# Softmax probabilities scaled on GpSimd before the transposes, instead of scaling the attention output

## The reference

```python
q = (query @ wq); k = (key @ wk); v = (value @ wv)     # heads of 128, rope on q and k
scores = jnp.einsum('bhqd,bhkd->bhqk', q, k) / scale
attn = jax.nn.softmax(scores + m[:, None, :, :], axis=-1)
out = jnp.einsum('bhqk,bhkd->bhqd', attn, v)
return out.reshape(bs, sq, HQ * DV) @ wo
```

## Time and profile before

| | us |
|---|---|
| three runs | 713.92, 716.35, 716.79 |
| median | 716.35 |
| the profiled execution | 712.92 |
| its span, first to last instruction | 711.2 |
| busy PE, PEld, DVE | 697.0, 592.6, 549.5 |
| busy ACT, POOL | 395.2, 300.5 |

### The profile page before, as it was taken

How to read it: one execution, slowest core, us unless ns; L and a number is a source line. 1 busy time by engine, 2 the same in 40 slices (tenths; PEclk the granted TensorE clock), 3 DMA queues, 4 the chain that set the end, 5 groups by cost and what they waited for, 6 DMA issues and landing times.

```text
span 711.2 us, 12231 instructions
## 1 busy us (share of the span) xinstructions
PE 697.0 (98%) x4085; PEld 592.6 (83%) x4085; DVE 549.5 (77%) x1175; ACT 395.2 (56%) x603; POOL 300.5 (42%) x151
## 2 busy tenths in 40 slices
PE   8999999999999999999999999999999999999986
PEld 7888888888888888888888888879989999999975
DVE  5988578658748857866865874767999999999994
ACT  4563454535546446345553654654867667676752
POOL 2353223404504503331340440200388887888780
DMA  8702022021001102202102100832887878788600
GB/s 310 271 30 75 1 74 74 0 74 59 15 22 59 66 0 74 74 0 74 64 9 74 59 0 0 348 157 79 338 292 285 339 301 340 298 336 301 282 7 16
DMA packets 20293, 93.77 MB, mean 132 GB/s; under 512 B 2608, under 2 KB 3760, under 8 KB 11440
## 3 DMA queue, kind: packets, MB, share of 16 engines
q1 hardware_dynamic: 20272, 93.50, 35.5%
HBM read 93.17 MB, written 0.33 MB: 131 GB/s over the span
## 4 chain that ended last, share of the span: by engine, by line
PE 91%; DVE 4%; DMA 3%; issue 1%; ACT 1%; SPq 0%; POOLq 0%; POOL 0%; DVEq 0%
PE bank L389 24%; PE bank L391 22%; PE bank L390 22%; PE bank L608 10%; PE bank L516 5%; PE bank L687 3%; DMA w_hs_sb<-in_w_hs 1%; DMA wqo_raw<-in_wq 1%; PE bank L487 1%; PE bank L396 1%; DVE decay L1291 1%; PE bank L443 1%; PE bank L696 1%; PE bank L659 1%; PE bank L736 1%
## 5 line engine op out<-in xcount | busy, mean ns | idle before, releaser
L1448 POOL TENSOR_TENSOR wqo_lo<-wqo_raw,wqo_hi 128x2048 fp32r<-128x2048 f32 x15 | 69.6, 4640 | 192.3 <-ACT wqo_hi L744 163.6
L1121 DVE TENSOR_TENSOR pt_lo<-bank,pt_hi 128x512 fp32r<-128x512 f32 x128 | 87.6, 689 | 51.6 <-ACT pt_hi L818 50.8
L818 ACT ACTIVATE pt_hi<-bank 128x512 fp32r<-128x512 f32 x128 | 75.6, 597 | 57.0 <-PE bank L516 57.0
L1435 POOL TENSOR_TENSOR k_lo<-rope_a,k_hi 128x512 fp32r<-128x512 f32 x32 | 42.8, 1338 | 104.2 <-ACT k_hi L762 104.2
L1082 DVE CUSTOM_DVE_ANT_0 probs<-bank,mask_sb 128x512 f32<-128x512 f32 x128 | 82.0, 686 | 0.1
L1481 POOL TENSOR_TENSOR w_out_lo<-w_out_sb,w_out_hi 128x2048 fp32r<-128x2048 f32 x16 | 73.5, 4591 | 16.2 <-ACT w_out_hi L931 16.2
L1486 POOL TENSOR_TENSOR w_gate_lo<-w_gate_sb,w_gate_hi 128x2048 fp32r<-128x2048 f32 x15 | 69.3, 4618 | 18.0 <-ACT w_gate_hi L923 18.0
L516 PEld LDWEIGHTS bank<-ident_r,probs_r 128*128 128x128 f32 x512 | 55.8, 140 | 19.2 <-DVE pt_lo L1121 5.1
L808 ACT ACTIVATE probs<-probs,neg_max 128x2048 f32<-128x2048 f32 x31 | 61.9, 2001 | 0.9 <-DVE neg_max L1072 0.8
L608 PE MATMUL bank<-xnT,w_hs_sb 128*128 128x128 f32 x512 | 60.6, 277 | 1.0 <-DMA w_hs_sb<-in_w_hs 1.0
L516 PE MATMUL bank<-ident_r,probs_r 128*128 128x128 f32 x512 | 57.8, 238 | 1.5 <-DVE pt_lo L1121 1.5
(11 more groups left out here) (193 smaller groups left out, 1728.2 us busy)
## 6 DMA issues: line engine op xcount, KB each, us to landing
w_hs_sb<-in_w_hs SPq DMA_DIRECT2D x16, 1024.0 KB, 4.8
w_gate_sb<-in_w_gate SPq DMA_DIRECT2D x16, 1024.0 KB, 4.8
w_out_sb<-in_w_out SPq DMA_DIRECT2D x16, 1024.0 KB, 6.3
wqo_raw<-in_wq SPq DMA_DIRECT2D x8, 1024.0 KB, 4.7
wqo_raw<-in_wo SPq DMA_DIRECT2D x8, 1024.0 KB, 4.8
decay<-decay_rows SPq DMA_DIRECT2D x16, 512.0 KB, 6.8
ctx_raw<-in_ctx_t SPq DMA_DIRECT2D x3, 1024.0 KB, 11.2
wk_raw<-in_wk SPq DMA_DIRECT2D x8, 256.0 KB, 2.7
```

Source lines behind the costliest of these rows:

```text
L818: act.activation(pt_hi[t % 3], ring_b[(t + 1) % 2][:, :], ACT.Copy).then_inc(s["pt_hi_ready"], 1)
L1121: dve.tensor_tensor(pt_lo[t % 3], ring_b[(t + 1) % 2][:, :], pt_hi[t % 3].bitcast(F32), ALU.subtract)\
L1448: pool.tensor_tensor(wqo_lo[:, :, :], wqo_raw[:, :, :], wqo_hi[:, :, :].bitcast(F32), ALU.subtract)\
```

## The change

In the first seven head groups VectorE inverts each head's row sum by itself (`inverse_row`, a 128 x 1 reciprocal), GpSimd multiplies that head's 128 x 2048 probabilities by it in place (`normalise`), and TensorE's transposes wait for this (`probs_normed`) where they waited for the exponentials. The two diagonals, the two broadcast matmuls, ScalarE's copy and `scale_out` are left out in these groups. `attn_high` and `attn_low` read `pv_bank`. The last group keeps the old way.

```diff
 def transpose_probs(g, t, last_head):
     if t == 0:
-        pe.wait_ge(s["probs_ready"], HG * (g + 1) - last_head)
+        if last_head:
+            pe.wait_ge(s["probs_ready"], HG * G - 1)
+        else:
+            pe.wait_ge(s["probs_normed"], HG * (g + 1))
...
-        if t == sum_steps(last_head)[2]:
-            if first_head(g) or not isinstance(g, int):
-                pe.wait_ge(s["ones_r_ready"], 1)
-            pe.wait_ge(s["diag_ready"], g + 1)
+        if last_head and t == SUM_STEPS[2]:
+            pe.wait_ge(s["ones_r_ready"], 1)
+            pe.wait_ge(s["diag_ready"], 1)
             pe.matmul(oq_bank..., ones_r, diag_hi...)
             pe.matmul(oq_bank..., ones_r, diag_lo...)
...
 def attn_high(g):
-    act.wait_ge(s["attn_out_ready"], g + 1)
-    act.activation(attn_hi[...], probs[:, 1, 0:512], ACT.Copy)
+    act.wait_ge(s["pv_ready"], g + 1)
+    act.activation(attn_hi[...], pv_bank[:, :], ACT.Copy)
...
 def q_and_k(g):
+    inverse_row(g - 1, 0)
+    inverse_row(g - 1, 1)
     k_rotate(g, 0)
+    inverse_row(g - 1, 2)
+    inverse_row(g - 1, 3)
     q_rotate(g)
     k_rotate(g, 1)
...
+def inverse_row(g, h):
+    dve.wait_ge(s["probs_ready"], HG * g + h + 1)
+    dve.reciprocal(inv_row[:, h:h + 1], row_sum[:, h:h + 1]).then_inc(s["inv_row_ready"], 1)
...
 pt_low(g, False)
-scale_out(g)
 v_low(g + 1, 0)
 attn_low(g)            # now reads pv_bank
...
+def normalise(g, h):
+    pool.wait_ge(s["inv_row_ready"], HG * g + h + 1)
+    keep_wait_apart(pool)
+    pool.tensor_scalar(probs[:, h, :], probs[:, h, :], inv_row[:, h:h + 1], None, ALU.mult)\
+        .then_inc(s["probs_normed"], 1)
...
 with pool.Fori(1, G) as g:
     split_wk(g)
     wqo_low(s["wq_hi_ready"], s["wq_lo_ready"], g)
     split_wv(g)
-    k_low(g)
+    normalise(g - 1, 0)
+    normalise(g - 1, 1)
+    k_low(g, 0)
+    normalise(g - 1, 2)
+    k_low(g, 1)
+    normalise(g - 1, 3)
+    k_low(g, 2)
+    k_low(g, 3)
     wqo_low(s["wo_hi_ready"], s["wo_lo_ready"], g - 1)
```

More of the change, by code:

```diff
@@ L53 @@
 LOWEST = -3.4028234663852886e38
-def sum_steps(last_head):
-    return (11, 12, 14, 15) if last_head else (1, 4, 7, 8)
+SUM_STEPS = (11, 12, 14, 15)
 def at_least(eng, sem, count):
@@ L150, in build @@
         row_sum = sb("row_sum", [P, HG], F32, attn)
+        inv_row = sb("inv_row", [P, HG], F32, attn)
         inv_hi = sb("inv_hi", [P, HG], F32R, attn)
@@ L256, in build @@
             qT_lo_ready vproj_ready v_copied vT_mm v_hi_ready v_lo_ready scores_ready scores_masked neg_max_ready
-            probs_ready pT_mm pt_hi_ready pt_lo_ready pv_ready inv_sum_ready inv_hi_ready inv_lo_ready diag_ready
+            probs_ready inv_row_ready probs_normed pT_mm pt_hi_ready pt_lo_ready pv_ready inv_sum_ready inv_hi_ready inv_lo_ready diag_ready
             bcast_mm bcast_ready attn_out_ready oproj_ready res_added small_in dequant_in dt_in gate_in0 gate_in1
@@ L750, in attn_high @@
             def attn_high(g):
-                act.wait_ge(s["attn_out_ready"], g + 1)
-                act.activation(attn_hi[:, :, :].rearrange("p h t -> p (h t)"), probs[:, 1, 0:512], ACT.Copy)\
+                act.wait_ge(s["pv_ready"], g + 1)
+                act.activation(attn_hi[:, :, :].rearrange("p h t -> p (h t)"), pv_bank[:, :], ACT.Copy)\
                     .then_inc(s["attn_hi_ready"], 1)
@@ L818, in pt_high @@
                     act.activation(pt_hi[t % 3], ring_b[(t + 1) % 2][:, :], ACT.Copy).then_inc(s["pt_hi_ready"], 1)
-                    if t == sum_steps(last_head)[3]:
-                        act.wait_ge(s["bcast_mm"], g + 1)
+                    if last_head and t == SUM_STEPS[3]:
+                        act.wait_ge(s["bcast_mm"], 1)
                         act.activation(probs[:, 2, 0:512], oq_bank[:, :], ACT.Copy).then_inc(s["bcast_ready"], 1)
@@ L880, in _ @@
             for i in range(2):
-                act.wait_ge(s["attn_out_ready"], G + i)
+                act.wait_ge(s["attn_out_ready"], i + 1)
                 act.activation(attn_hi[:, 2 * i:2 * i + 2, :].rearrange("p h t -> p (h t)"),
@@ L1090, in mask_scores, with last_inverse_sums, last_inverse_sums_low @@
                 row_max(g, HG - 1)
[L1092 to L1100, removed]
+            def inverse_row(g, h):
+                dve.wait_ge(s["probs_ready"], HG * g + h + 1)
+                dve.reciprocal(inv_row[:, h:h + 1], row_sum[:, h:h + 1]).then_inc(s["inv_row_ready"], 1)
+            def last_inverse_sums():
+                dve.wait_ge(s["probs_ready"], HG * G - 1)
+                dve.wait_ge(s["last_exp"], KB)
+                dve.tensor_reduce(row_sum[:, HG - 1:HG], block_max[:, HG - 1, :], X_AXIS, ALU.add)\
+                    .then_inc(s["last_sum_ready"], 1)
+                dve.wait_ge(s["last_sum_ready"], 1)
                 dve.reciprocal(inv_sum, row_sum[:, :]).then_inc(s["inv_sum_ready"], 1)
-                dve.wait_ge(s["inv_sum_ready"], g + 1)
+                dve.wait_ge(s["inv_sum_ready"], 1)
                 dve.tensor_scalar(inv_hi[:, :], inv_sum, 1.0, None, ALU.mult).then_inc(s["inv_hi_ready"], 1)
-                dve.wait_ge(s["inv_hi_ready"], g + 1)
+                dve.wait_ge(s["inv_hi_ready"], 1)
                 dve.tensor_tensor(inv_lo, inv_sum, inv_hi[:, :].bitcast(F32), ALU.subtract)\
                     .then_inc(s["inv_lo_ready"], 1)
-                dve.wait_ge(s["k_lo_ready"], KB * (g + (1 if last_head else 2)))
+                dve.wait_ge(s["k_lo_ready"], KB * G)
                 dve.tensor_tensor(diag_hi[:, :, :], ident[:, :].unsqueeze(1).broadcast_to([P, HG, P]),
                                   inv_sum.unsqueeze(2).broadcast_to([P, HG, P]), ALU.mult)
-            def inverse_sums_low(g):
-                dve.wait_ge(s["inv_lo_ready"], g + 1)
-                dve.wait_ge(s["pT_mm"], KT * g + 1)
+            def last_inverse_sums_low():
+                dve.wait_ge(s["inv_lo_ready"], 1)
+                dve.wait_ge(s["pT_mm"], KT * (G - 1) + 1)
                 dve.tensor_tensor(diag_lo, ident[:, :].unsqueeze(1).broadcast_to([P, HG, P]),
@@ L1122, in pt_low @@
                         .then_inc(s["pt_lo_ready"], 1)
[L1123 to L1132, removed]
+                    if last_head and t == SUM_STEPS[0]:
+                        last_inverse_sums()
+                    if last_head and t == SUM_STEPS[1]:
+                        last_inverse_sums_low()
             def add_out(g):
@@ L1140, in attn_low @@
                 dve.wait_ge(s["attn_hi_ready"], g + 1)
-                dve.tensor_tensor(attn_lo[:, :, :].rearrange("p h t -> p (h t)"), probs[:, 1, 0:512],
+                dve.tensor_tensor(attn_lo[:, :, :].rearrange("p h t -> p (h t)"), pv_bank[:, :],
                                   attn_hi[:, :, :].rearrange("p h t -> p (h t)").bitcast(F32), ALU.subtract)\
@@ L1197, in _ @@
             pt_low(G - 1, True)
-            dve.wait_ge(s["bcast_ready"], G)
+            dve.wait_ge(s["bcast_ready"], 1)
             dve.wait_ge(s["pv_ready"], G)
@@ L1429, in split_weight, with k_low @@
                     .then_inc(lo_done, 1)
[L1431 to L1437, removed]
+            def k_low(g, b):
+                blk = slice(b * 512, (b + 1) * 512)
+                pool.wait_ge(s["k_hi_ready"], KB * g + b + 1)
+                pool.tensor_tensor(k_lo[:, blk], rope_a[:, (b + 1) % 2, :], k_hi[:, blk].bitcast(F32), ALU.subtract)\
+                    .then_inc(s["k_lo_ready"], 1)
+            def normalise(g, h):
[3 more added lines that the diff above has]
+                    .then_inc(s["probs_normed"], 1)
             def split_wk(g):
@@ L1467, in _ @@
             split_wv(0)
-            k_low(0)
+            for b in range(KB):
+                k_low(0, b)
             with pool.Fori(1, G) as g:
```

## The result

The changed kernel takes 787.41 us (median of four runs, 786.08 to 788.38) against 715.41 for the kernel before in the runs measured with it: ratio 1.1017, interval 1.0984 to 1.105. The forecast was 723.5 and slower, the range 712 to 738. The sign was right, the size was wrong by a factor of ten (72 us against 7).

What follows compares the result with a forecast made beforehand. TensorE's matmuls were taken as the bound. Stalls of 0.52 and 1.03 less 0.53 saved gave +1.0 us an iteration, +7.1 for seven: 723.5 against the median 716.35, range 712 to 738.

Steps and rivals of the forecast that it cites:

- The bound, the saving: TensorE's matmuls bound the loop; leaving out the broadcast matmuls saves 0.53 us an iteration, 3.7 for seven.
- The lock: A VectorE addition of two SBUF tiles meeting a running GpSimd instruction waits for its end, then needs 0.55 us more.
- steps 2 to 4: Held VectorE rotation additions cost TensorE 0.52 us before turning q and 1.03 at the third turned block, each iteration.
- step 3: At q's rotation, its addition waits for GpSimd's K low part, hiding the reciprocals; q ends at 232.15 against 231.63.
- D: Time of one GpSimd normalise of 2048 columns, taken as 1.9 us from the cast, bounds 1.89 and 4.58.
- Step 5: TensorE's new wait for probs_normed: head 3 done at 239.65, TensorE there at 240.42 + 0.52, so no cost.
- rival D: A slower GpSimd normalise: at 3 us each, +23, 746; at 4.58 TensorE waits for head 3, over 770; chance 0.12.
- The sum's formula: Cost of the held additions per iteration, 3D - 4.15 us, with D the time of one GpSimd normalise.
- A: VectorE's additions get past a running normalise, both stalls vanish and 3.7 us stay as gain: 712.6; chance 0.21.
- B: Near cancellation: normalise takes 0.9 to 1.7 us, or a margin behind k_rotate(3) was counted too low: 716; chance 0.14.
- C: GpSimd keeps the lock, so q's addition waits for head 2 too: 13 us on top, 736.5; chance 0.13.

Runs made afterwards that it cites:

- half-width kernel: The changed kernel with only 1024 of 2048 columns of each head multiplied by the inverse sum: 720.56 us, ratio 1.0078.
- two-input pair: The changed kernel with normalise as a two-input tensor_tensor, inverse sum broadcast: 762.03 us; the same with both rotations' additions reading PSUM: 728.15 us.
- the saving alone: The changed kernel without the four normalisations, TensorE waiting for the exponentials as before: 709.84 us, ratio 0.9911.
- the quarter: The changed kernel with only the first 512 of 2048 columns of each head multiplied by the inverse sum: 708.71 us, ratio 0.99.
- PSUM additions: The changed kernel with the cosine products of both rotations written back to PSUM, so VectorE's additions read PSUM and one SBUF tile: 787.29 us, ratio 1.0998.

## Why the prediction was right or wrong

- **The bound, the saving** (the part on the broadcast matmuls): right. 3.7 us foretold (0.53 for an iteration), 4.3 measured by the iterations (0.61). The parts priced at nothing, `scale_out`, the diagonals and the reciprocals, cost nothing. The second pair of reciprocals is hidden by the low part of K block 0, as step 3 had it.
- **The lock**: right in kind. All three additions named in steps 2 to 4 are held, and a fourth too. The half-width kernel shows its price without anything else, and the two-input pair gives it at 3.6 us, 28 to 34 us. One of the three places that I read it from doesn't fit: the normalised x ends at 6.27, only 0.28 us behind the cast, and takes 0.545 by itself, so that it was let go before the cast's end. That already spoke against a hold to the end for one-input instructions.
- **The term that failed is D in "`normalise` in"**: "the cast is nearest: D = 1.9 us", with 4.58 as the upper bound. It measures 5.45, above both ends. The error was to take a cast as the measure of another one-input operation and the two-input subtraction as a ceiling. Neither is an end of a range for an operation with no row of its own. The rate of the GPSIMD Engine Reference of the Trainium skill (Performance versus the Vector engine), 1.8 cycles an element as the best case, was off in the same direction: the estimate from it, 3.07 us, is closer, and still far under 5.45.
- **Step 5, the wait priced at nothing**, is what D then turned over. With 1.9 us GpSimd's queue has pauses; with 5.45 it has none, and 4 of them with two K low parts and the weights make 30.8 us where 21.7 were free. That is 9.1 of the 10.2 us. The parts other than the normalisations are 9.0 us of it, so the chain alone outgrows the 21.7 us from D = 3.2 on, an estimate from these rows; at 3.6 it was 23.38. That lies inside my own bounds. So the direction came out right, but the additions, which I had it from, were not what set the time. I had seen this in rival D ("TensorE would also wait for head 3: over 770") but gave it no chance of its own.
- **The sum's formula** 3D - 4.15 counts the lock alone. At 3.6 us it gives 759 with the saving, and 762 was measured; at 5.45 it gives 798 and 787 was measured, since there the chain is the bound; at 2.85 it gives 3.9 us an iteration with the saving and 1.1 was measured. The additions get through 1.74 us early there, which the steps don't have. That the agreement at 3.6 us is more than luck isn't shown: there the chain and the clock have a part too.
- **TensorE's clock** was left out. Behind the start of the q weight's low part, TensorE's first turned block comes 30.85 us later (249.79 to 280.64) instead of 21.70, 9.15 more; the rest of the iteration takes 37.39 us instead of 36.30. That 1.09 is the clock's loss less the saving, which is 0.61 by the iterations of the saving alone: 1.7 us for the clock, as 3.4 us at half speed would cost and as the iteration without a fall shows above. So 9.15 for the chain and 1.7 for the clock, less 0.61 saved, make the 10.24 us.
- **The rivals**: A is excluded: in the kernel after four additions of an iteration were held, each until 1.74 us before the normalisation's end. B needed a D of at most 1.7. (At the quarter's 1.56 us the steps leave a loss of 0.69 in an iteration against the gain of 0.53, and no loss came.) C is excluded by the half-width kernel; the sign that I gave for it, TensorE idle over 2 us before turning q, came with 3.4 us, from D. D was the true case. It had 0.12, and its times lay outside the range.

## What to carry to other kernels

Price an operation on GpSimd only from a row of that very operation; where there is none, the range has to reach well beyond the slowest row in sight, and the duration at which the engine's queue loses its last pause belongs in the text as a threshold. When work goes to another engine, lay out that engine's whole queue up to the consumer: the free time between its first input and the consumer's due time counts (21.7 us here), not its mean load of 31%. Here the pauses of ScalarE, each long enough for one copy with a scale, were the right place, and short instructions that read two SBUF tiles should not stand beside long ones on GpSimd.

## What the runs showed of the hardware that was not expected

- On GpSimd, in float32, 128x2048, a `tensor_scalar` multiplication is slower than `tensor_tensor`: 5.45 us against 4.64 for a subtraction of two full inputs and 3.60 with the second broadcast; with a constant 5.37.
- A held VectorE addition goes ahead of a GpSimd instruction that stands behind the running one, and that one then takes 0.4 us longer.
- `tensor_scalar` lets the addition go 1.74 us before its reported end, at 1024 columns and at 2048; the two-input forms and the K low parts don't. Why was not tried.
- TensorE's 14 pauses of 2.95 to 4.09 us in the loop of the kernel after were each followed by a stretch at half clock. Behind the one shown this was 3.4 us, which began about 0.5 us after work resumed (0.59, 0.50, 0.50 and 0.70 in four stretches of 1 us). Of 21 pauses of 1.75 to 2.03 us in the loops of the two-input kernels 12 were followed by such a stretch and 9 were not; those of 1.09 to 1.30 us (half width) left the clock at 1.00.
- In the pause of 9.29 us (PSUM additions) the granted clock fell to 0.50 while TensorE was still idle. The mean clock of an execution counts that too: 0.952 there against 0.965 in the kernel after, at the same time.
